# Layer-one input rows: the normalisation leaves GpSimd, ScalarE forms the high halves from raw rows, VectorE the low halves in two operations

## The reference, cut to what matters

```
def _layernorm(x, axis=-1, eps=1e-05):
    m = jnp.mean(x, axis=axis, keepdims=True)
    v = jnp.var(x, axis=axis, keepdims=True)
    return (x - m) / jnp.sqrt(v + eps)

def _gcn_conv(x, W, b, src, dst, n):
    h = x @ W
    ...
    deg = jax.ops.segment_sum(jnp.ones_like(dst_sl, dtype=h.dtype), dst_sl, num_segments=n)
    dinv = jnp.where(deg > 0, jax.lax.rsqrt(deg), 0.0)
    norm = dinv[src_sl] * dinv[dst_sl]
    msgs = h[src_sl] * norm[:, None]
    out = jax.ops.segment_sum(msgs, dst_sl, num_segments=n)
    return out + b

h = _gcn_conv(_layernorm(x), W1, b1, src, dst, N_NODES)
```

## Time and profile before

| quantity | us |
|---|---|
| median of 3 runs (2289.72 to 2290.46) | 2290.35 |
| profiled execution, device time | 2288.68 |
| its span, first to last instruction | 2287.0 |
| TensorE busy / share of span | 2104.1 / 92% |
| VectorE busy / share of span | 1577.0 / 69% |
| ScalarE busy / share of span | 819.5 / 36% |
| GpSimd busy / share of span | 474.3 / 21% |

### The profile page before, as it was taken

One profiled execution on the slowest core, in us unless ns is written; L12 is line 12 of the kernel. 1 busy time (PEld: TensorE's weight loads), 2 busy tenths in 40 slices (PEclk: granted clock), 3 DMA queues, 4 the chain that ended last, 5 costly groups with the idle time before them and its releaser, 6 DMA issues. The chain is left out here.

```text
span 2287.0 us, 43796 instructions
## 1 busy us (share of the span) xinstructions
PE 2104.1 (92%) x14031; PEld 1416.2 (62%) x14032; DVE 1577.0 (69%) x5153; ACT 819.5 (36%) x1862; POOL 474.3 (21%) x628
## 2 busy tenths in 40 slices
PE   1599999999999999679999999998299999999997
PEld 1256666666666666335555555554189999999996
DVE  7899999999999999223444434344766666666664
ACT  4544444444444444201111212112054444444442
POOL 3600000000000000000000000000055655565653
PEclk9999999999999999889999999999599999999998
DMA  6022222222222222154655566673423332332322
GB/s 192 30 85 85 85 114 85 85 113 86 85 103 96 86 94 105 59 203 168 211 185 189 207 227 225 209 244 111 173 53 48 50 50 47 49 49 47 52 48 27
DMA packets 73895, 255.02 MB, mean 112 GB/s; under 512 B 10407, under 2 KB 50792, under 8 KB 59528
## 3 DMA queue, kind: packets, MB, share of 16 engines
q1 hardware_dynamic: 31160, 181.37, 21.0%
q0 software_dynamic: 28464, 58.79, 12.0%
q10 hardware_dynamic: 14112, 12.85, 1.6%
HBM read 137.89 MB, written 115.08 MB: 111 GB/s over the span
## 5 line engine op out<-in xcount | busy, mean ns | idle before, releaser
L677 PE MATMUL mp_o<-rows,m_counts 128*128 128x512 f16 x2401 | 597.8, 380 | 2.9 <-ACT m_counts L783 1.7
L1526 PE MATMUL rp_o<-rows,r_adj 128*128 128x512 f16 x2401 | 551.1, 380 | 33.5 <-DMA r_adj<-adj 33.5
L597 DVE TENSOR_SCALAR m_oh_cell<-m_cells,m_edge_cell 128x246 f16<-128x246 f16 x2500 | 521.8, 284 | 0.0
L775 ACT ACTIVATE m_counts<-mp 128x490 f16<-128x490 f32 x586 | 339.3, 583 | 461.7 <-PE mp L712 461.6
L1526 PEld LDWEIGHTS rp_o<-rows,r_adj 128*128 128x128 f16 x2401 | 235.5, 99 | 282.1 <-issue 36.6
L712 PE MATMUL mp<-m_oh_cell,m_oh_lane 128*128 128x245 f16 x2500 | 366.1, 272 | 27.5 <-DVE m_oh_cell L597 17.9
L677 PEld LDWEIGHTS mp_o<-rows,m_counts 128*128 128x128 f16 x2401 | 233.0, 97 | 188.5 <-issue 7.3
L712 PEld LDWEIGHTS mp<-m_oh_cell,m_oh_lane 128*128 128x128 f16 x2500 | 245.5, 99 | 163.4 <-DVE m_oh_cell L597 17.1
L2018 PE MATMUL fp_h<-f_xt,w 128*128 128x256 f16 x2688 | 304.5, 274 | 0.2 <-DVE f_xt L2114 0.2
L2037 PE MATMUL fp_y<-w,f_hh 128*128 x2688 | 302.4, 273 | 0.0
L2018 PEld LDWEIGHTS fp_h<-f_xt,w 128*128 x2688 | 263.9, 98 | 31.2 <-issue 0.6
(11 more groups left out here) (213 smaller groups left out, 1633.5 us busy)
## 6 DMA issues: line engine op xcount, KB each, us to landing
adj<-m_counts SPq DMA_DIRECT2D x49, 1568.0 KB, 5.2
r_adj<-adj SPq DMA_DIRECT2D x49, 1568.0 KB, 6.7
r_raw<-in_L_ffn_W_dram POOLq DMA_DIRECT2D x16, 1024.0 KB
w_parts<-r_parts POOLq DMA_DIRECT2D x8, 1024.0 KB, 5.7
w<-w_parts SPq DMA_DIRECT2D x4, 2048.0 KB
rows<-in_x_dram SPq DMA_DIRECT2D x7, 896.0 KB, 11.2
r_x<-in_x_dram SPq DMA_DIRECT2D x49, 128.0 KB, 2.0
out_dram<-r_x ACTq DMA_DIRECT2D x49, 128.0 KB, 1.7
```

Source lines behind the costliest of these rows:

```text
L597: oh = nc.vector.tensor_scalar(oh_cell[:, slot(n) + i, :], cells[:], edge_cell[:, item:item + 1], None, ALU.is_equal)
L677: mm = nc.tensor.matmul(ps_o[q], counts[:, q, s, :], k.rows[0][:, s, :], start=i == 0, stop=i == BLOCKS - 1)
L775: last = nc.scalar.activation(counts[:, q, :, lo - b * P:hi - b * P].rearrange("p h (a d) -> p h a d", d=STEP), halves, ACT.Copy, scale=CO ...
L1526: mm = nc.tensor.matmul(ps_o[q], adj[:, q, s * P:(s + 1) * P], rows[:, s, :], start=s == 0, stop=s == BLOCKS - 1)
```

## The change

GpSimd's 49 normalising operations and its wait for the scales go. When `inv` (one over the root of the degrees) is there, VectorE multiplies `rstd` and `shift` by it and by 64, in place. ScalarE makes the high halves from the raw rows with these as scale and shift (`Identity` in place of `Copy`), without a wait on `z_done`. VectorE makes the low halves in two operations: `xs = xs*rstd - high`, in fp32 and in place, then `low = xs + shift`, to fp16. Both run in groups of three: three of the first, then three of the second, which wait on `z_done`, now counted up by the first ones.

```
-                pool.wait_ge(scales_ready, 1)
-                for r in range(BLOCKS):
-                    nc.gpsimd.tensor_scalar(xs[:, r, :], xs[:, r, :], rstd[:, r:r + 1], shift[:, r:r + 1], ALU.mult,
-                                            ALU.add).then_inc(z_done, 1)
...
             def lows(rows):
                 for r in rows:
                     dve.wait_ge(hi_done, r + 1)
-                    nc.vector.scalar_tensor_tensor(k.rows[0][:, r, D:2 * D], xs[:, r, :], k.dinv_in[:, r:r + 1],
-                                                   k.rows[0][:, r, 0:D], ALU.mult, ALU.subtract).then_inc(lo_done, 1)
+                    nc.vector.scalar_tensor_tensor(xs[:, r, :], xs[:, r, :], rstd[:, r:r + 1], k.rows[0][:, r, 0:D],
+                                                   ALU.mult, ALU.subtract).then_inc(z_done, 1)
+                for r in rows:
+                    dve.wait_ge(z_done, r + 1)
+                    nc.vector.tensor_scalar(k.rows[0][:, r, D:2 * D], xs[:, r, :], shift[:, r:r + 1], None,
+                                            ALU.add).then_inc(lo_done, 1)
...
                         nc.vector.tensor_scalar(k.dinv_in[:], inv[:], SCALE, None, ALU.mult).then_inc(dinv_ready, 1)
+                        nc.vector.scalar_tensor_tensor(rstd[:], inv[:], SCALE, rstd[:], ALU.mult, ALU.mult).then_inc(dinv_ready, 1)
+                        nc.vector.scalar_tensor_tensor(shift[:], inv[:], SCALE, shift[:], ALU.mult, ALU.mult).then_inc(dinv_ready, 1)
                         nc.vector.tensor_scalar(k.dinv_out[:], inv[:], 1.0 / (SCALE * COUNT_SCALE), None,
                                                 ALU.mult).then_inc(dinv_ready, 1)
                     if n == DEG_AT + 1:
-                        dve.wait_ge(dinv_ready, 2)
+                        dve.wait_ge(dinv_ready, 4)
...
                     if n == DEG_AT + 1:
-                        act.wait_ge(dinv_ready, 2)
+                        act.wait_ge(dinv_ready, 4)
                     for r in rows_at(n):
-                        act.wait_ge(z_done, r + 1)
-                        nc.scalar.activation(k.rows[0][:, r, 0:D], xs[:, r, :], ACT.Copy,
-                                             scale=k.dinv_in[:, r:r + 1]).then_inc(hi_done, 1)
+                        nc.scalar.activation(k.rows[0][:, r, 0:D], xs[:, r, :], ACT.Identity, bias=shift[:, r:r + 1],
+                                             scale=rstd[:, r:r + 1]).then_inc(hi_done, 1)
```

## The result

The changed kernel takes 2294.26 us (median of 13 runs, 2292.52 to 2298.91); the kernel before, on the same chips, 2290.35 us (13 runs, 2288.55 to 2293.09). The ratio is 1.0018, with an interval of 1.0010 to 1.0027: slower by 2 to 6 us, a little under the 0.2% named in the prediction. The profiled execution took 2292.74 us with a span of 2291.0 us, against 2288.68 and 2287.0 before.

The account below looks back on a forecast made before the run. VectorE's last low half, which releases TensorE's backlog, was taken to set the end. -2.98 - 0.69 - 4.8 + 12.9 + 0.5 = +4.9 us on 2290.35 gave 2295.3 us, range 2291.3 to 2301.4.

Parts of the forecast that it names:

- (a): Banks 0 to 6, before the degrees: VectorE undisturbed by GpSimd gains 2.98 us; the wait for the root keeps its length.
- (b): Reciprocal to next `oh_lane`: eight cheaper `oh_cell` save 0.89 us, two small operations add 0.20 us; gain 0.69 us.
- (c): Banks 9 to 24, the part beside GpSimd, to 104 us: VectorE's operations no longer stretched, gain 4.8 us.
- (d): VectorE's 49 added low-half operations at 0.263 us each cost 12.9 us; bounds 9.5 and 19.5 us.
- (f): GpSimd's first self-loop addition, at 104 us before, can come when bank 12 is emptied; worth nothing.
- (e): ScalarE's high halves with two per-row numbers: up to 0.11 us more each, hidden behind VectorE's longer bank.
- clock term: TensorE's half-clock stretch may fall behind the handover near 131 us: costs 0 to 1.8 us, taken as 0.5.
- the slow rate: Rival: VectorE's added operation runs at 0.397 us, 6.6 us on top, 2301.9 us; chance 0.07.
- something other than GpSimd stretches VectorE: Rival: before 104 us, transfers for example; gains (a) to (c) are lost, +13.4 us, 2303.7 us; chance 0.05.
- ScalarE didn't set the pace: Rival judged: ScalarE's two-number high halves take over 0.75 us each and set the pace; at 0.85, 2300 us; chance 0.03.
- a new operation under 0.173 us: Faster rival: VectorE's added operation costs less than that, so the change pays; at 0.13 us, 2288.3 us; chance 0.05.
- The second rival: Added operation nearer 0.194 us, or clock free and (c) gains slightly more: +1.0 to +4.4 us, 2291.4 to 2294.8; chance 0.12.

Follow-up runs that it names:

- second comparison: The changed kernel run again unaltered, against the kernel before: 2295.40 us (11 runs), ratio 1.0020.
- the last experiments: Changed kernel with idle TensorE products: three behind each of banks 16 to 23, 2297.26 us; two behind each and eight behind bank 24, 2295.22 us.

## Why the prediction held

The forecast was 2295.3 us and the measured median is 2294.26: 3.9 us over before, where the sum had 4.9. In the second comparison it was 5.5 us (2295.40 against 2289.90). By its steps:

(a) Banks 0 to 6 got 2.98 us cheaper by the sum, and the reciprocal came 3.43 us earlier (81.36 to 77.93). The extra is, but for 0.06 us by which bank 0 started earlier, the wait for the root, 1.53 us in place of 1.92, which the prediction had kept. TensorE's four products of bank 6 and the transpose of the degrees show why, first before, then after:

```profile
79.54 0.98 PE L712 MATMUL mp<-m_oh_cell,m_oh_lane 128*128 128x245 f16 x4 [1.04 <-issue]
80.45 0.34 PE L718 MATMUL mp_o<-ident,m_deg_t 49*128 49x49 f32 x1
```

```profile
76.50 0.59 PE L714 MATMUL mp<-m_oh_cell,m_oh_lane 128*128 128x245 f16 x4 [1.09 <-DVE m_oh_lane L590]
77.02 0.26 PE L720 MATMUL mp_o<-ident,m_deg_t 49*128 49x49 f32 x1
```

They ran at the full clock this time; in the run without the second operation, whose streams are the same up to there, they take 0.98 us and the wait is 1.92 us again. So this term moves by 0.4 us from one execution to the next. (The granted clock is given as 1.00 for this window of before, though the products ran at half speed: up to 104 us that column doesn't fit the products in this trace, so it isn't used there.)

(b) From the reciprocal to the next `oh_lane` it is 2.48 us (77.93 to 80.41), against 3.14: 0.66 in place of 0.69 us.

(c) and (d) Between that `oh_lane` and the last low half the changed kernel takes 130.63 - 80.41 = 50.2 us, before 126.39 - 84.50 = 41.9: 8.3 us more, where the sum had 12.9 - 4.8 = 8.1. The new operation goes at 0.263 us (three from 83.24 to 84.03), as L519's row had said, so the step from fp32 to fp16 doesn't lose the faster rate. The 0.2 us that the sum missed is in bank 13. GpSimd's first self-loop now falls beside VectorE's `oh_cell` of that bank, four of which take 1.11 us in place of 0.86; the prediction had called it worth nothing (f):

```profile
93.15 1.11 DVE L597 TENSOR_SCALAR m_oh_cell<-m_cells,m_edge_cell 128x246 f16<-128x246 f16 x4
93.21 0.58 POOL L434 TENSOR_TENSOR m_counts<-m_counts,self_loop 128x128 f16<-128x128 f16 x1 [51.88 <-ACT m_counts L785]
```

(e) The high half with two per-row numbers lasts 589 ns, within the 0.57 to 0.61 expected, and VectorE waits for nothing between banks 9 and 24. The 93 ns per operand of the Trainium skill ("ScalarE: Activation LUTs", section "What ACT_TABLE_LOAD costs") agree with the step from 498 to 589 ns, 91 ns.

```profile
L799 ACT ACTIVATE rows<-rows,m_shift,m_rstd 128x256 f16<-128x256 f32 x49 | 25.6, 589 | 0.0
```

Without the clock term the sum said +4.4 us at the handover, and it is +4.24; part of this closeness is luck, since 0.4 us of a shorter wait and 0.25 us for the self-loop, both left out of the sum, offset each other in part. (g) The clock term was given at 0 to 1.8 us and taken at 0.5. The profiles show nothing in the first and 1.25 us in the second. How often a run has the low stretch isn't known, so the 0.5 is neither borne out nor refuted, and the last experiments show that the clock at the handover doesn't explain the spread of the runs.

The chances were less good than the sum. Slower by over 0.2% had 0.57 and within 0.2% had 0.38; the ratio of 1.0018, and 1.0020 in the second comparison, lies just inside 0.2%, and its interval reaches over it. With a forecast of 2295.3 the two should have been closer.

Of the rivals, the slow rate (+6.6 us) was built as an experiment and lengthened the stretch by 6.6 us, and the one in which something other than GpSimd stretches VectorE fell with the run in which an idle GpSimd was given other work. ScalarE didn't set the pace, as VectorE never waited for its high halves, and a new operation under 0.173 us is out at 0.263. The second rival isn't told from the forecast by the time: 2294.26 us lies in both ranges. Its first half, an operation near 0.194 us, is out; its second half, a clock that costs nothing, is what the first profile shows and the second doesn't.

## What to carry to other kernels

An operation given to GpSimd isn't free for VectorE: here each cost it 0.17 us on average, and nothing where VectorE was waiting anyway, so bringing one back to VectorE pays only if its cost there is lower, and at 0.263 us it isn't. Compare the surcharge with the price of the work, both as steps from one start to the next on the engine that sets the end; an engine that has idle time and whose work leaves VectorE's pace alone is the better home (ScalarE here: with GpSimd silent and ScalarE at work, four `oh_cell` keep their 0.86 us). Where VectorE hands over to TensorE's backlog, count to the last operation that the backlog waits for, since everything behind it moves as one piece.

## What the runs showed of the hardware

- A GpSimd operation on fp32 rows, one every 0.72 us, costs VectorE 0.17 us on average while VectorE has work, on the rows and on an unrelated buffer alike; VectorE isn't stopped for the operation's full length (0.62 us). It hits 16-bit one-tensor operations (0.194 to 0.305 us), the fp32 to fp16 one (0.88 to 1.16 us for three) and two-tensor ones (1.26 to 1.49 us for three L548 before).
- An operation that reads fp32 and writes fp16 with one per-row number goes at the same 0.263 us as one with 32-bit numbers in and out (L519 before).
- Two executions of the same kernel, equal to 0.01 us up to the handover, differ by 1.25 us in the next 20 us: TensorE's clock fell to half in one of them, behind 1.98 us of idle time, and stayed full in the other, behind 1.76 us. In one profile with that idle time filled it stayed full. The clock alone doesn't account for the 4 to 6 us between runs.
